# Low-rank A fetched later, one base block through VectorE, B gathered sooner: a routed low-rank layer and an FFN on one core

## What is computed

```python
# layer 0: adapter of the sequence, then base + routed low-rank
c    = einsum('bsi,boi->bso', x, L0_cond_weight[ids])          # 16 adapters of 1024 x 1024
logits = c @ W_router.T                                        # 8 experts, top 2, softmax
h    = einsum('td,erd->ter', c, lora_A)                        # rank 16
x    = x + c @ W_base.T + b_base + 2 * einsum('ter,eor,te->to', h, lora_B, w)
# layer 1: mix per sequence, then an FFN per head over permuted features
y    = einsum('bct,bcd->bdt', x, L1_cond_weights[ids])
x    = x + unpermute(down(gelu(up(permute(y)))))
```

## Time and profile before

| | |
|---|---|
| median of 3 runs | 611.19 us |
| the profiled execution | 612.55 us |
| its span, first to last instruction | 610.7 us |
| granted TensorE clock, mean | 0.999 |
| TensorE busy | 593.5 us, 97% |
| VectorE, ScalarE, GpSimd busy | 77%, 24%, 21% |

### The profile page before, as it was taken

One profiled execution on the slowest core, in us unless ns is written; L12 is line 12 of the kernel. 1 busy time (PEld: TensorE's weight loads), 2 busy tenths in 40 slices (PEclk: granted clock), 3 DMA queues, 4 the chain that ended last, 5 costly groups with the idle time before them and its releaser, 6 DMA issues.

```text
span 610.7 us, 13500 instructions
## 1 busy us (share of the span) xinstructions
PE 593.5 (97%) x4383; PEld 349.0 (57%) x4384; DVE 471.6 (77%) x1303; ACT 144.7 (24%) x290; POOL 128.5 (21%) x195
## 2 busy tenths in 40 slices
PE   4999999999998999989999999999999999999997
PEld 3344444344433444457767676767676767676773
DVE  3068778878887779698888897879987889887863
ACT  3100000200020002154333523225342325231324
POOL 4010002121111220060022231313131313131312
PEclk9999999999999999999999999999999999999999
DMA  8998998998999987111022222222232223231322
GB/s 264 407 394 315 309 301 293 325 312 301 315 409 402 355 310 254 44 59 39 17 65 90 74 87 71 87 71 91 63 94 68 88 64 97 62 93 60 94 72 86
DMA packets 43427, 106.90 MB, mean 175 GB/s; under 512 B 8450, under 2 KB 17666, under 8 KB 43394
## 3 DMA queue, kind: packets, MB, share of 16 engines
q1 hardware_dynamic: 30914, 76.04, 36.0%
q0 software_dynamic: 6784, 21.51, 10.6%
q10 hardware_dynamic: 5696, 8.95, 4.3%
HBM read 98.09 MB, written 8.39 MB: 174 GB/s over the span
## 4 chain that ended last, share of the span: by engine, by line
PE 86%; DVE 6%; DMA 4%; issue 1%; DVEq 0%; SPq 0%; ACTq 0%; POOL 0%; another core or an unknown queue 0%
PE wide L546 26%; PE bank L653 20%; PE bank L661 10%; PE bank L741 8%; PE wide L724 8%; PE y_wide L577 4%; DVE c_pair L1108 3%; DMA ring<-adapters_dram 3%; PE y_wide L699 3%; PE wide L561 2%; DMA x_in<-x_seq_dram 1%; PE bank L674 1%; PE bank L677 1%; PE bank L673 1%; PE bank L754 1%
## 5 line engine op out<-in xcount | busy, mean ns | idle before, releaser
L546 PE MATMUL wide<-ring,x_in 128*64 128x512 f32 x960 | 209.5, 592 | 1.8 <-DMA ring<-adapters_dram 1.5
L546 PEld LDWEIGHTS wide<-ring,x_in 128*64 128x64 f32 x960 | 73.0, 137 | 126.7 <-issue 126.7
L1306 DVE STREAM_TRANSPOSE x_tok<-xres 32x128 f32<-32x128 f32 x464 | 140.3, 302 | 6.0
L1108 DVE STREAM_TRANSPOSE c_pair<-wide 32x256 f32<-32x256 f32 x240 | 107.1, 446 | 39.5 <-issue 22.1
L955 ACT ACTIVATE act_sb<-wide 128x512 f32<-128x512 f32 x120 | 66.3, 608 | 191.3 <-PE wide L724 191.3
L653 PE MATMUL bank<-c_hi,base_t 128*128 128x512 f32 x384 | 102.3, 390 | 0.0
L430 POOL DMA_INDIRECT xres<-xT_dram,row_in x32 | 34.3, 1073 | 230.1 <-DVE out_sb L1296 226.8
L653 PEld LDWEIGHTS bank<-c_hi,base_t 128*128 128x128 f32 x384 | 71.9, 188 | 15.4
L661 PE MATMUL bank<-c_lo,base_t 128*128 (+1 forms) x256 | 78.0, 390 | 0.0
L468 POOL COPY c_all<-c_pair 128x512 f32 x30 | 19.4, 672 | 213.7 <-DVE c_pair L1108 213.7
L870 ACT ACTIVATE small<-small 128x1 f32<-128x1 f32 x16 | 3.2, 203 | 218.2 <-DVE small L1144 218.2
(11 more groups left out here) (166 smaller groups left out, 605.1 us busy)
## 6 DMA issues: line engine op xcount, KB each, us to landing
ring<-adapters_dram SPq DMA_DIRECT2D x128, 512.0 KB, 5.9
x_in<-x_seq_dram ACTq DMA_DIRECT2D x32, 256.0 KB, 4.9
down_sb<-down_dram SPq DMA_DIRECT2D x32, 128.0 KB
up_raw<-up_dram SPq DMA_DIRECT2D x62, 64.0 KB
ar_sb<-lora_a_router_dram ACTq DMA_DIRECT2D x1, 544.0 KB, 4.3
mix_sb<-mix_dram SPq DMA_DIRECT2D x32, 16.0 KB
xres<-xT_dram,row_in POOLq DMA_INDIRECT x32, 3.4
out_dram<-out_sb,row_out POOLq DMA_INDIRECT x28, 2.9
```

Of the source, the lines that this page charges most:

```text
L546: last = pe.matmul(acc[half][h][z * TOK:(z + 1) * TOK, :], x_in[:, half, z, k, :], ring[:, k, z, h * HALF:(h + 1) * HALF], start=(k == 0), ...
L1108: last = nc.vector.transpose(c_pair[r * SQ:(r + 1) * SQ, :, q * SQ:(q + 1) * SQ], wide[half][q * SQ:(q + 1) * SQ, :, :] .rearrange("p h (k ...
L1306: last = nc.vector.transpose(x1_tok[q * SQ:(q + 1) * SQ, :].rearrange("p (c f) -> p c f", f=P)[:, :, f * SQ:(f + 1) * SQ], xres[f * SQ:(f ...
```

## The change

- `SOON` goes from 5 to 4: four base blocks are gathered and transposed ahead of pair 0. The fifth is gathered into `raw_tile` once x of pair 0 has landed, transposed by VectorE before it turns pair 0 (`turn_tile(-1, ...)`), and copied by ScalarE (`tile_kept(-1)`) before x of pair 2 is loaded. `LOOPED` (3) is the number of blocks left for the loop, which ran three times before too.
- The fetch of low-rank A moves on ScalarE's queue from the start to behind x of pair 1.
- `BUSY` goes from 8 to 4. A copy of one column on ScalarE comes before the wait for the list, and with it the load of the table.
- `GATHERS`: B and the bias are gathered after pairs 1 to 8 instead of 4 to 11.
- `turn_four` is cut: its first four transposes come at the end of the pair before.
- VectorE's `last_seqs` moves ahead of `turn_pair` of pair 14.

```diff
-SOON = 5
-BUSY = 8
+SOON = 4
+LOOPED = KT - SOON - 1
+BUSY = 4
-GATHERS = range(PAIRS // 4, PAIRS // 4 + KT)
+GATHERS = {j + 1: (j,) for j in range(KT)}
...
+            pool.wait_ge(x_in_in[0], 32)
+            on_its_own()
+            gather(raw_tile[:, :], w_base, perm_sb[:, SOON:SOON + 1], tile_in)
             pool.wait_ge(order_ok, 1)
             for t in range(PAIRS - 1):
                 keep_pair(t)
-                if t % 4 == 0 and t // 4 < KT - SOON:
-                    j = t // 4 + SOON
-                    if t > 0:
-                        pool.wait_ge(tile_turned, t // 4)
+                if t % 4 == 0 and t // 4 < LOOPED:
+                    j = t // 4 + SOON + 1
+                    pool.wait_ge(tile_turned, t // 4 + 1)
                     gather(raw_tile[:, :], w_base, perm_sb[:, j:j + 1], tile_in)
-                if t in GATHERS:
-                    j = t - GATHERS[0]
+                for j in GATHERS.get(t, ()):
                     gather(b_rows[:, j, :], lora_b, perm_sb[:, j:j + 1], b_in)
...
-            act.dma_start(ar_sb[:, :, :], lora_a_router.rearrange("(k p) e -> p k e", p=P)).then_inc(ar_in, 16)
...
             act.sem_inc(hw_placed, 8)
+            act.wait_ge(ident_ok, 2)
+            nc.scalar.copy(th, ident[:, 0:1])
             act.wait_ge(lists_ok, 1)
             load_x(0, 0)
             for j in range(SOON):
                 base_copied(j)
             load_x(1, 1)
+            act.dma_start(ar_sb[:, :, :], lora_a_router.rearrange("(k p) e -> p k e", p=P)).then_inc(ar_in, 16)
+            tile_kept(-1)
             for half in range(2):
                 next_x(half, half)
                 tanh(half)
...
+            turn_tile(-1, range(0, 16))
             turn_pair(0, 0)
             route(0)
-            with dve.Fori(0, KT - SOON) as i:
+            with dve.Fori(0, LOOPED) as i:
                 for n in range(4):
                     t = i * 4 + 1 + n
                     turn_pair(t, (n + 1) % 2)
                     if n < 3:
                         turn_tile(i, TILE_PIECES[n])
                     else:
-                        turn_four(i)
+                        turn_four(i, range(1, 4))
                     route(t, hw_four[:, (n + 1) % 4, :])
+                    if n == 2:
+                        turn_four(i, range(0, 1))
             pair(PAIRS - 3, 1)
+            seqs = last_seqs(dve)
             turn_pair(PAIRS - 2, 0)
```

More of the change, by code:

```diff
@@ L895, in tile_kept @@
             def tile_kept(i):
-                act.wait_ge(tile_turned, i + 1)
-                nc.scalar.copy(base_rows[:, bass.ds(i + SOON, 1), :, :].rearrange("p a k o -> p (a k o)"), c_tok[:, :]) \
+                act.wait_ge(tile_turned, i + 2)
+                nc.scalar.copy(base_rows[:, bass.ds(i + SOON + 1, 1), :, :].rearrange("p a k o -> p (a k o)"), c_tok[:, :]) \
                     .then_inc(base_turned, 1)
@@ L918, in _ @@
                 tanh(half)
-            with act.Fori(0, KT - SOON) as i:
+            with act.Fori(0, LOOPED) as i:
                 for n in range(4):
@@ L1186, in turn_tile @@
                 if pieces[0] == 0:
-                    dve.wait_ge(tile_in, (i + 1) * 16)
-                    dve.wait_ge(base_turned, i + SOON)
+                    dve.wait_ge(tile_in, (i + 2) * 16)
+                    dve.wait_ge(base_turned, i + SOON + 1)
                 for n in pieces:
@@ L1195, in turn_tile, with turn_four @@
                     last.then_inc(tile_turned, 1)
[L1197 to L1202, removed]
+            def turn_four(i, qs):
+                if qs[0] == 0:
+                    dve.wait_ge(hw_ok, i * 4 + 4)
+                    dve.wait_ge(hw_placed, i * 8 + 8)
+                for q in qs:
                     for r in range(P // SQ):
@@ L1205, in turn_four @@
                                                    hw_four[r * SQ:(r + 1) * SQ, :, q * SQ:(q + 1) * SQ])
-                last.then_inc(hw_turned_ok, 1)
+                if qs[-1] == P // SQ - 1:
+                    last.then_inc(hw_turned_ok, 1)
             def pair(t, half):
@@ L1227, in _ @@
                 base_rest(j)
-            seqs = last_seqs(dve)
             hw_turned(PAIRS - 3)
```

## The result

The changed kernel takes 619.68 us (median of 4 executions, 618.92 to 621.19) beside 611.40 for the kernel before in the same runs (4, 611.18 to 611.63): a ratio of 1.0138, 95% interval 1.0118 to 1.0159. Forecast: slower, 613.7, with a range up to 617.2. The direction came out, and so did the cause, A landing late behind a wait. The size did not: the measured time lies outside the range.

A forecast was written before the change was run, and what follows sets the result against it. TensorE, busy 97%, was taken as the bound. Span 610.7 + 3.2 (A) - 0.5 (transposes) - 0.2 (B's gathers) = 613.2; against the median 611.19 + 2.5 = 613.7 us. Own range 612.4 to 616.3; 8 in 10, 608.6 to 617.2.

The forecast's parts named there:

- The fetch of A: Before pair 1: A, issued behind x of pair 1, lands at 35.3 and starts pair 1 3.2 us later.
- the one for one: On the DMA engines: A's packets alternate singly with adapter packets, so A's 64 per engine take 11.7 us.
- so A has landed ... and waits 4.7 us; pair 1 starts 3.2 us later: Before pair 1: A landed at 35.3, TensorE ready at 30.6; bounds for the delay +0.4 to +5.8 us.
- rival 3: TensorE's clock falls to half rate in the wait for A: +2.4 us, 616.1 us, chance 0.13.
- The fall ahead of pair 0: In the gap before pair 0, growing from 1.01 to some 2.8 us: a clock fall hidden by the wait for A.
- x of pair 0: At the start: without the fifth gather x lands sooner, pair 0 starts at 16.8; -1.5 us, bounds 0 to -2.1.
- My own sign of being wrong: At pair 0: a first adapter matmul still at 18.3 would show the forecast wrong.
- rival 2: At pairs 0 and 1: x comes no sooner, or A is only just late; 610.5 to 610.9 us, chance 0.13.
- The fifth block through VectorE: Around pair 0: gather issued at 16.9, landed at 23.2, transposed till 30.2, before pair 0's end; costs nothing.
- The cut of the transposes: At the router after a fourth pair: moving four transposes earlier removes TensorE's wait at 119.22; -0.46 us.
- B's gathers: Around 188 us: gathers starting 3 pairs sooner relieve the crowded stretch; -0.2 of the 1.28 us adapter wait.
- Rival 1: Before pair 1: A's small packets pass in a run, landing at 26.7; 609.0 us, faster, chance 0.32.

The follow-up runs named there:

- e4: Changed kernel with low-rank A laid out as 128 rows of 4352 bytes, same bytes in 128 packets instead of 1024: 613.19 us, ratio 1.0025.
- e8: Changed kernel with low-rank A fetched in two DMAs of 68 columns each, 2048 packets of 272 bytes: 623.50 us, ratio 1.0194.
- e7: Changed kernel with TensorE's two register reads for pair 1 ahead of the wait for A instead of behind it: 616.92 us, ratio 1.0076.
- e12: Changed kernel with 36 filler transposes ahead of pair 0 and 40 before the wait for A: 617.82 us, ratio 1.0112.
- e6: Run e1 with the first adapter rows held back until both halves of x of pair 0 are issued: 610.65 us, ratio 0.9988.
- e1: Changed kernel with the fetch of A back at the start of ScalarE's queue: 612.32 us, ratio 1.0017.
- e5: Run e1 with 36 filler transposes instead of 4 ahead of pair 0: 612.11 us, ratio 1.0016.
- e9: Kernel before with only the cut of turn_four, its first four transposes at the end of the pair before: 611.69 us, ratio 1.0004.
- e10: Kernel before with only the first adapter rows held back until both halves of x of pair 0 are issued: 610.08 us, ratio 0.9984.

## Why the prediction was wrong

- **The fetch of A** (term +3.2): the mechanism was right. A went out at 16.18 (forecast near 16) and took 20.35 us (19 forecast), and the one for one of the earlier trace rows holds for packets of 544 bytes too, and of 272. e4 and e8 change the number of packets with the bytes kept, and the landing moves with it.
- **The step that failed is "so A has landed ... and waits 4.7 us; pair 1 starts 3.2 us later"**. It measured 6.2. Two things are in the gap. A landed at 36.5, 1.2 later than forecast: its first packet came at 22.1, sooner than my 23.3, but from first to last they took 13.8 us and not 11.7. I had put the fifth block's gather ahead of A's packets; it ran among them and took near a third of the turns from 23 to 26 us. And I let pair 1 start with A's landing, though two register reads stand between the wait and the first matmul: 1.75 us, confirmed by e7. The code was in front of me, and the trace of before shows nothing of them as a cost because there the sequencer had run ahead.
- **The clock** I had as rival 3 with a chance of 0.13 and a price of 2.4: it fell, for 2.2 us. e12 shows the 2.2 apart from the wait. The fall ahead of pair 0, which I had named as hidden by the wait for A, came too (1.7 us) and was hidden. My chance was too low by my own row: in the earlier trace rows 2.5 us without a matmul (606.9 to 609.4) stood ahead of a fall, and I forecast a wait of 4.7; the fall belonged in the main case. 6.2 + 2.2 = 8.4 at the first router. The forecast also took off 0.7 further on, of which the medians show next to nothing: 3.0 + 2.2 + 0.7 = 5.9 us, against the 6.0 between 613.7 and the measured 619.7.
- **x of pair 0** (term -1.5): it started 0.15 to 0.7 us sooner in the eight profiles with four blocks ahead and the adapter rows issued as before. My own sign of being wrong, a first matmul still near 18.3, was there. The low end of the bounds, as in rival 2, was near the truth. The fifth gather gave its 1.7 us at x's first packet, and the turns with the adapter rows took them back before its last (e6). It did not matter to the changed kernel, as forecast, and made e1 a loss instead of a gain.
- **The fifth block through VectorE** (nothing): the zero is right for the changed kernel, my sum for it is not. I took 6.3 us for its gather from a less crowded stretch and issued it at 16.9; from 18.86 it took 8.4, and VectorE was done with pair 0 at 41.88, after a router at 30.6 + 8.6 = 39.2 would have come. Only the wait for A, which I had named as a further spare, covered it. e5 shows the 0.83 us it costs once nothing else waits.
- **The cut of the transposes** (-0.46): there was nothing to win, and e9 measures no effect. I had priced a single wait of one execution, behind a stray one.
- **B's gathers** (-0.2): the crowded pair around 190 us, router to router, took 17.6 to 17.9 us in the four profiles with the old places and 17.0 to 17.6 in the ten with the new ones. It fits, but was not tried alone; it stays open.
- **Rival 1**, that A's small packets get through in a run, is refuted by the packet counts and times of the changed kernel and of e8. The Trainium skill, "DMA: Bandwidth & Descriptors", section on queues, rings and completion order, has an engine drain 9 to 17 descriptors before it turns; here it turned after each one (1.75 adapter packets at the end of an A packet against 0.92 by chance, and no A packets beyond chance), also where one queue had 64 or 128 in line. The measurement decides.

## What to carry to other kernels

Cost a transfer that shares the DMA engines with a backlog by its packets, not its bytes: a table in short runs belongs where the engines are free, or in long rows (4.3 us at the start, 20.35 us beside the adapter rows, 11.2 in long rows there). Put a wait right ahead of the first use, and register reads ahead of the wait, not behind it. A wait on TensorE of some microseconds can have a second price, the slower clock after it, which can be checked by keeping the engine busy with useless transposes.

## What the hardware showed that I had not expected

- A DMA engine alternated single packets between two queues at all three pairs of sizes seen here: 146 to 146 (2048 and 4096 bytes), 368 to 370 (544 and 4096), 695 to 694 (272 and 4096). The same 0.56 MB took 11.2 us to land in 128 packets and 20.35 in 1024, in the same place of the queue.
- After 4.07 us without work the clock was at 0.50 in e1's profile, though at 1.00 during those 4 us; but not in every execution: of e1's ten, three had a mean clock of 1.000. So the level shown in an idle stretch did not say at which level the next work would run.
- Holding back 4 MB of adapter rows by 1.1 us (first issue at 10.77 instead of 9.69) made the kernel 1.0 us faster (e10): the small transfer that shares the engines with them, x, was the one waited for.
